# Gated linear attention on one core: inverse norms of q spread over the partitions by DMA instead of TensorE transposes

## The reference

```python
q = l2norm((x @ Wq).reshape(B, T, 8, 128))      # u / max(sqrt(sum(u*u)), 1e-12), per head and position
k = l2norm((x @ Wk).reshape(B, T, 8, 128))
v = (x @ Wv).reshape(B, T, 8, 128)
alpha = sigmoid(x @ Wg).reshape(B, T, 8, 128)
# for each t:  S = alpha_t * S + k_t v_t^T ;  o_t = S^T q_t
x = layernorm(x + o @ Wo)
x = layernorm(x + ffn(x))
```

## Time and profile before

| what | value |
|---|---|
| median of 3 runs | 1853.79 us (1848.47 to 1857.78) |
| the profiled execution | 1857.98 us |
| its span, first to last instruction | 1856.2 us |
| PE busy | 1725.2 us, 93% of the span |
| DVE busy | 1462.5 us, 79% |
| ACT busy | 1077.9 us, 58% |
| POOL busy | 600.1 us, 32% |
| chain of work that ended last | PE 77%, DVE 11%, issue 6%, ACT 4%, DMA 0% |
| mean granted PE clock | 0.987 of full |
| SP's DMAs in the attention | 16 loads of x_nat, 256 KB each, median 3.5 us to landing |

### The profile page before, as it was taken

How to read it: one execution, slowest core, us unless ns; L and a number is a source line. 1 busy time by engine, 2 the same in 40 slices (tenths; PEclk the granted TensorE clock), 3 DMA queues, 4 the chain that set the end, 5 groups by cost and what they waited for, 6 DMA issues and landing times.

```text
span 1856.2 us, 81900 instructions
## 1 busy us (share of the span) xinstructions
PE 1725.2 (93%) x35719; PEld 1425.5 (77%) x35719; DVE 1462.5 (79%) x3391; ACT 1077.9 (58%) x2355; POOL 600.1 (32%) x474
## 2 busy tenths in 40 slices
PE   6999999999999999999999999999789999999996
PEld 5788887878878788887878888878667777777775
DVE  4878887888888778787887888788768787878786
ACT  5665555656656655665566566555455656565553
POOL 2322222232223223222322322232234444444444
PEclk9999999999999999999999999999989999999999
DMA  7000000000000000000000000000000000000000
GB/s 211 4 10 9 4 9 4 10 4 9 10 4 9 4 9 4 9 9 4 9 4 9 4 10 9 4 9 3 3 12 13 22 20 16 24 12 24 13 17 12
DMA packets 28657, 26.99 MB, mean 15 GB/s; under 512 B 1928, under 2 KB 23696, under 8 KB 28304
## 3 DMA queue, kind: packets, MB, share of 16 engines
q1 hardware_dynamic: 28304, 21.77, 3.9%
HBM read 13.38 MB, written 4.19 MB: 9 GB/s over the span
## 4 chain that ended last, share of the span: by engine, by line
PE 77%; DVE 11%; issue 6%; ACT 4%; DMA 0%; POOL 0%; DVEq 0%; SPq 0%; POOLq 0%; ACTq 0%
PE bank L527 11%; PE bank L529 10%; PE bank L528 10%; PE bank L660 8%; PE bank L615 7%; PE bank L670 5%; PE bank L646 5%; PE bank L618 5%; PE bank L567 5%; PE bank L577 4%; PE bank L634 3%; PE bank L603 3%; ACT v_sb L979 2%; DVE v_sb L1531 2%; DVE s_sb L1528 1%
## 5 line engine op out<-in xcount | busy, mean ns | idle before, releaser
L458 POOL TENSOR_TENSOR rn_sb<-ss_sb,expo 128x8 f32<-128x8 f32 x128 | 213.4, 1668 | 783.2 <-DVE ss_sb L1287 783.2
L1242 DVE TENSOR_TENSOR qq_sb<-qq_sb,tot_sb 128x512 f32<-128x512 f32 (+1 forms) x384 | 264.2, 688 | 189.5 <-PE bank L615 150.1
L1242 DVE TENSOR_TENSOR k_sb<-k_sb,tot_sb 128x512 f32<-128x512 f32 (+1 forms) x384 | 322.8, 841 | 4.7 <-PE bank L618 4.5
L1004 ACT ACTIVATE at_sb<-diag_sb 32x256 f32<-32x256 f32 x256 | 106.0, 414 | 171.6 <-DVE diag_sb L1254 166.9
L979 ACT ACTIVATE v_sb<-bank,rn_sb 128x128 f32<-128x128 f32 x512 | 139.1, 382 | 82.0 <-PE bank L529 78.5
L615 PEld LDWEIGHTS bank<-qq_sb,k_sb 128*32 128x32 f32 x12288 | 128.6, 110 | 59.6 <-issue 44.9
L615 PE MATMUL bank<-qq_sb,k_sb 128*32 128x16 f32 x12288 | 149.7, 185 | 23.2 <-issue 21.6
L968 ACT ACTIVATE a_sb<-bank 128x512 f32<-128x512 f32 x128 | 76.3, 597 | 154.1 <-PE bank L529 145.7
L660 PE MATMUL bank<-v_sb,at_sb 128*128 128x128 f32 x1024 | 151.6, 291 | 4.4 <-DVE res L1294 2.5
L495 POOL TENSOR_TENSOR wq_lo<-v_sb,wq_hi 128x512 fp32r<-128x512 f32 x80 | 104.7, 1308 | 138.0 <-ACT wq_hi L1127 138.0
L1120 ACT ACTIVATE sq_sb<-bank 128x512 f32<-128x512 f32 x160 | 95.4, 597 | 86.2 <-PE bank L529 85.7
(11 more groups left out here) (203 smaller groups left out, 4366.2 us busy)
## 6 DMA issues: line engine op xcount, KB each, us to landing
x_nat<-in_L_attn_x_dram SPq DMA_DIRECT2D x16, 256.0 KB, 3.5
x_nat<-x_all SPq DMA_DIRECT2D x16, 256.0 KB, 2.4
out_dram<-k_sb SPq DMA_DIRECT2D x16, 256.0 KB, 2.3
ew_raw<-in_L_ffn_exp_w_dram SPq DMA_DIRECT2D x3, 512.0 KB, 5.0
qq_sb<-in_L_attn_Wq_dram SPq DMA_DIRECT2D x1, 512.0 KB, 4.1
qq_sb<-in_L_attn_Wk_dram SPq DMA_DIRECT2D x1, 512.0 KB, 6.4
k_sb<-in_L_attn_Wg_dram SPq DMA_DIRECT2D x1, 512.0 KB, 7.2
k_sb<-in_L_attn_Wv_dram SPq DMA_DIRECT2D x1, 512.0 KB
```

The source lines that it names most:

```text
L458: nc.gpsimd.tensor_tensor(rn_sb[par][:, i, :, :].rearrange("p h c -> p (h c)"), ss_sb[:, i * G:(i + 1) * G], expo[:, 0:G], ALU.pow).then_i ...
L1242: return nc.vector.tensor_tensor(view, view, by, ALU.mult)
```

## The change

The eight transposes of a slot become one: PE transposes the 128 x 8 tile `rn_sb` as it is into 8 rows of 128 (`turn_norms`), ACT copies these 8 x 128 numbers into `nr_sb` (`take_norms`), SP stores them as 4 KB in memory (`nr_dram`), waits for that, and loads the 4 KB back into each of the 128 partitions of `nb_sb` (512 KB written). DVE then multiplies all of q by `nb_sb` in one instruction of 128 x 1024, now placed behind the growth for j = 6. The load of x for later batches is issued from the same SP loop, no longer from a loop of its own.

```diff
+        nr_sb = sb("nr_sb", [G, C])
+        nb_sb = sb("nb_sb", [128, W])
+        nr_dram = nc.dram_tensor("nr_dram", (2, G, C), fp32, kind="Internal").ap()
...
-            with sp.Fori(1, B) as b:
-                next_x(b)
+            def spread_norms(P):
+
+                rows = nr_dram[P % 2]
+                sp.wait_ge(rr_evac, P + 1)
+                sp.dma_start(rows, nr_sb[:, :]).then_inc(nr_out, 16)
+                sp.wait_ge(nr_out, (P + 1) * 16)
+                await_count(sp, qn_done, P)
+                sp.dma_start(nb_sb[:, :], bass.AP(rows.tensor, rows.offset, [[0, 128], [1, W]])).then_inc(nr_in, 16)
+
+            for P in range(B * NP):
+                spread_norms(P)
+                if P == 0:
+                    next_x(1)
+                if P % NP == NP - 1 and P // NP + 2 < B:
+                    next_x(P // NP + 2)
...
-            def spread_norms(par, P):
+            def turn_norms(par, P):
 
                 pe.wait_ge(rn_done, P * 2 + 1)
-                await_count(pe, s_done, (P - 1) * HP * (NC - 1))
-                for h, bank in enumerate((nb_ps, kt_ps)):
-                    for c in range(NC):
-                        mm = nc.tensor.transpose(bank[:, c * C:(c + 1) * C],
-                                                 rn_sb[par][:, 0, h, c:c + 1].to_broadcast([128, 128]), ident[:, :])
-                    mm.then_inc(rb_full, 1)
+                nc.tensor.transpose(nb_ps[0:G, C:2 * C], rn_sb[par][:, 0, :, :].rearrange("p h c -> p (h c)"), ident[:, :]).then_inc(rr_full, 1)
...
                     scores(par, P, 5)
+                    if has_next:
+                        turn_norms(1 - par, P + 1)
                     if has_prev:
                         outputs_of_state(prev_p, P - 1, 0)
                     if has_next:
                         sums_of_squares(P + 1, 1, n_x)
-                        spread_norms(1 - par, P + 1)
                     scores(par, P, 6)
...
+            def take_norms(P):
+
+                act.wait_ge(rr_full, P + 1)
+                await_count(act, nr_out, P * 16)
+                nc.scalar.activation(nr_sb[:, :], nb_ps[0:G, C:2 * C], ACT.Copy).then_inc(rr_evac, 1)
...
                         take_gate(1 - par, P + 1)
+                        take_norms(P + 1)
                     spread_diagonal(par, P)
...
-            def normalise_q(par, P, h):
-                dve.wait_ge(rb_full, P * HP + h + 1)
-                seg = q_sb[par][:, h * T:(h + 1) * T]
-                nc.vector.tensor_tensor(seg, seg, (nb_ps, kt_ps)[h][:, :], ALU.mult).then_inc(qn_done, 1)
+            def normalise_q(par, P):
+                dve.wait_ge(nr_in, (P + 1) * 16)
+                nc.vector.tensor_tensor(q_sb[par][:, :], q_sb[par][:, :], nb_sb[:, :], ALU.mult).then_inc(qn_done, 1)
...
-                        if j == 6 and has_next:
-                            for h in range(HP):
-                                normalise_q(1 - par, P + 1, h)
-
...
                     if has_next:
+                        normalise_q(1 - par, P + 1)
                         own_products(1 - par, P + 1)
```

More of the change, by code:

```diff
@@ L226, in gated_linear_attention_and_moe_block @@
         rn_done = sem("rn_done")
-        rb_full = sem("rb_full")
+        rr_full = sem("rr_full")
+        rr_evac = sem("rr_evac")
+        nr_out = sem("nr_out")
+        nr_in = sem("nr_in")
         qn_done = sem("qn_done")
@@ L369, in next_x @@
                 sp.wait_ge(xt_full, b)
-                sp.dma_start(x_nat[:, :, :], x[bass.ds(b, 1)].rearrange("a (c t) d -> t (a c) d", t=C)).then_inc(xn_in, 16)
-            with sp.Fori(1, B) as b:
-                next_x(b)
+                sp.dma_start(x_nat[:, :, :], x[b].rearrange("(c t) d -> t c d", t=C)).then_inc(xn_in, 16)
+            def spread_norms(P):
[11 more added lines that the diff above has]
+                    next_x(P // NP + 2)
             def ffn_io(b, first=False, last=False):
@@ L514, in transposes_of_x @@
                 pe.wait_ge(xn_in, (n + 1) * 16)
-                await_count(pe, qn_done, n * NP * HP - 1)
+                await_count(pe, rr_evac, n * NP)
                 for c in range(NC):
@@ L557, in sums_of_squares @@
                     pe.wait_ge(x_lo, n_x)
-                    await_count(pe, qn_done, P * HP)
+                    await_count(pe, rr_evac, P)
                 else:
@@ L626, in transposes_of_k @@
                     pe.wait_ge(k_up, (P + 1) * 6)
-                    if not last:
-                        pe.wait_ge(qn_done, (P + 2) * HP)
+                    await_count(pe, s_done, P * HP * (NC - 1))
                 else:
@@ L723, in _ @@
             sums_of_squares(0, 1, 1)
-            spread_norms(0, 0)
+            turn_norms(0, 0)
             for n in range(2):
@@ L1041, in _ @@
             take_gate(0, 0)
+            take_norms(0)
             for n in range(2):
@@ L1210, in own_products @@
             def own_products(par, P):
-                dve.wait_ge(qn_done, (P + 1) * HP)
+                dve.wait_ge(qn_done, P + 1)
                 await_count(dve, qk_full, (P - 1) * STEPS + 1)
@@ L1358, in _ @@
             dve.wait_ge(const_dve, 5)
-            for h in range(HP):
-                normalise_q(0, 0, h)
+            normalise_q(0, 0)
             own_products(0, 0)
```

## The result

| | before | after |
|---|---|---|
| median | 1854.66 us (4 runs) | 1917.89 us (4 runs, 1911.08 to 1923.22) |
| profiled span | 1856.2 us | 1914.0 us |
| mean granted PE clock | 0.987 | 0.975 |

The ratio is 1.0343, 95% interval [1.0299, 1.0387]: slower by 63 us, where +48 was forecast; the time lies inside the range.

What follows compares the result with a forecast made beforehand. PE was taken to bound the kernel. Slots +29, work queued behind DVE's wait +7 and the start +12 summed to +48 us: 1906 us profiled, 1902 us against the median, range 1855 to 1985.

Steps and rivals of the forecast that it cites:

- allowance: Time in a slot between PE's turning of the norms and `scores(1)` of the next slot: mean 9.27 us.
- The new chain: From the turn through store, load and DVE to `scores(1)`: 9.73 us, 0.46 us longer than the allowance.
- 29 + 7: Costs given to slots: 29 us for the longer chain, 7 us for work queued behind DVE's wait.
- PE's own work: Seven of eight transposes go, 0.89 us a slot, leaving PE's path from turn to `scores(1)` at 8.38 us.
- The trip hides: Rival: store and load together cost 3.5 us instead of 5.0, PE stays the bound, 1814 us; chance 0.07.
- W + R: W, the store without its bytes, 1.56 us, plus R, the load into 128 partitions, 3.44 us.
- Its neighbour: Rival: W + R between 4.1 and 4.5 us, time about 1858 us or just below; chance 0.07.
- The one-row read is slow: Rival: loading the same 4 KB into all 128 partitions takes 5.1 us, total 2007 us; chance 0.13.
- DVE and POOL get in each other's way: Rival: the new multiplication loses 0.42 us beside a POOL product, +26 us, 1928 us; chance 0.05.
- The place on DVE: DVE's growths of j = 6 are no part of the chain, ending near 619 us, norms arriving near 620.1.
- Queued behind DVE's wait: DVE instructions behind the normalisation delay a new batch's first projection by 0.5 us in 15 slots, +7 us.
- The start: The first store of norms stands behind all the starting loads on SP: first `scores(1)` at 45.5 us, +12 us.

Runs made afterwards that it cites:

- e7: The changed kernel, its load bringing only the first head's norms (256 KB), which scale both heads: 1900.93 us, ratio 1.0208.
- e2: The changed kernel without the store of the norms and its wait; the load reads 4 KB of Wq instead: 1857.31 us, ratio 1.0030.
- e10: e9 with seven transposes a slot put back on PE, whose result nobody reads: 1876.29 us, ratio 1.0080.
- e6: The changed kernel, its load taking 128 different rows of Wq instead of one row for all partitions: 1921.35 us, ratio 1.0329.
- e3: The changed kernel with the turning transpose moved ahead of the second half of the gates' projection: 1863.08 us, ratio 1.0080.
- e9: The changed kernel with the edits of e1 and e3 together: 1870.89 us, ratio 1.0048.
- e8: The changed kernel with the normalisation back ahead of the growths of j = 6: 2011.06 us, ratio 1.0826.
- e4: The kernel before, with only its normalisation moved behind the growths of j = 6: 1849.93 us, ratio 1.0004.
- e1: The changed kernel, with the norms of slot 0 alone spread by the eight transposes of before: 1903.13 us, ratio 1.0286.
- e12: The kernel before, with sums of squares over 128 positions at once instead of four times 32: 1933.77 us, ratio 1.0408.
- e11: e9 with sums of squares over 128 positions at once instead of four times 32: 1910.40 us, ratio 1.0288.
- e5: The changed kernel with the store of the norms issued twice in series, each awaited: 2030.52 us, ratio 1.0931.

## Why the prediction was right, and where it was off

**What bounds the kernel.** Right. The kernel was bound by PE with a short DVE tail behind the norms, and the trip through memory became the chain that sets `scores(1)`. The allowance of 9.27 us from four slots is 9.22 over all 62.

**The new chain.** Means over 62 slots, the forecast by the prediction's own terms:

| step, us | forecast | measured |
|---|---|---|
| turn to the store's issue | 0.27 + 0.28 + 0.17 | 0.60 |
| store to the load's issue | 1.56 + 0.17 | 1.51 |
| load to the normalisation | 3.44 + 0.05 | 3.72 |
| normalisation to `scores(1)` | 1.20 + 2.49 + 0.10 | 4.07 |
| sum | 9.73 | 9.90 |

Each step is within 0.3 us. The store had the right sum by luck: 1.24 with its hop in 46 of 64 slots, 2.3 on average in the other 18. The load's 3.44 was near (3.6), but its parts weren't: e7 shows 0.4 for 256 KB, not 0.74, so more of it is fixed. DVE's part was 0.3 short; `scores(1)` came 3.91 after the normalisation in the median slot, not 3.79, and later where POOL's product was met. The forecast was +0.46 a slot; the slot grew by 0.63, 39 us against the 29 + 7 I gave to slots. That these two sums are so near is in part luck: of the 7 only 3 came, and the 6 that the part up to the outputs grew by were not in the sum.

**PE's own work.** This is the step that failed, though it left the sum alone, since DVE ends last. I priced eight transposes at 0.89 us a slot, called PE's gain certain, and let `scores(6)` come 0.89 earlier. From the first outputs to `scores(6)` the mean went from 2.91 to 2.35 us only, the median from 2.53 to 2.31. Before, `scores(6)` started 0.46 us (median) after DVE's growth of k for j = 5 had ended; the least that any kernel shows is 0.10. So there was 0.36 us of slack behind that growth, and PE now waits out the rest in 39 of 60 slots; the whole 0.89 counts only where a gap behind an instruction packet had made PE late, which is why the mean fell by more than the median. The growth takes 1.53 us beside POOL's first product of the gates in both kernels. Where the trip hides (e2), a third of a microsecond is lost again behind `scores(6)` (6.64 us to `scores(1)`, 6.31 before), where the normalisation now meets POOL, and the slots gain 0.22. Putting the work back (e10) costs 0.1 a slot by the medians, 0.19 in the profile. I also wrote that the wait at the edge would hide PE's "issue" gaps; those behind instruction packets went only from 41.9 to 37.0 us. And since PE loses part of its gain before the edge, it waits there 0.9 us a slot (55 us in 60), not the 1.3 I named as a sign.

**The rivals.** "The trip hides" needed W + R under 4.2. It was 1.34 + 3.6 = 4.9, and even at 3.7 (e2) the time is 1857 and not 1814, because PE waits for DVE ahead of `scores(6)` and of `scores(1)` instead. Its neighbour, W + R from 4.1 to 4.5, was put at 1858 or just below; at 4.5 my own terms give -0.04 x 63 + 19 = +16, 1870. "The one-row read is slow" falls by e6. "DVE and POOL get in each other's way" happens in 18 of 63 slots of the change, at 0.38 us each, 7 us in all and not 26: in the others POOL's product has ended before the norms arrive, as I said, or ends within 0.2 us of it. In e2, e3 and e9 it is nearly every slot. The rule of a fixed 2.0 us and bytes / 436e3 would have 2.01 for the store and 3.20 for the load, estimates from the Trainium skill, "DMA: Bandwidth & Descriptors", section "Anatomy of one DMA — SWDGE (gpsimd) path". That section is on DMAs issued by GpSimd, which I didn't say, and these are issued by SP. Here the store's issue to the load's is 1.24, and the load is 3.6. For 256 KB the rule says 0.6, e7 0.4.

**The place on DVE.** That the growths of j = 6 are no part of the chain is right: with them in it (e8) the time is 90 us more, and the move by itself costs nothing (e4).

**Queued behind DVE's wait.** The first projection of a new batch starts 1.65 us after `scores(1)`, 1.44 before (15 slots each): +0.21, 3 us in all where I said 7. What covers the rest of the four DVE instructions I did not resolve. The delayed masks cost nothing that shows: the part of the slot up to the outputs grew by 0.10, as much as the turn now ahead of them takes (0.11 from 647.01 to the outputs).

**The start.** Forecast 45.5 and +12 (9 to 14), measured 45.12 and +13.4; e1 takes it away. The store did wait for the loads ahead of it.

**What was not in the sum.** The second half, "untouched", took 5.2 us longer: the same code at a granted clock of 0.97, 0.98 before. 13.4 + 39.2 + 5.2 = 57.8 us is the whole difference of the spans. The medians are 63 apart; the rest is from run to run.

## What to carry to other kernels

A spread over partitions by a store of 4 KB and a load of 512 KB costs 5 us from the first issue to landing, so it must start that long before its use, or not at all on an edge where the slack is 1 us. Before work is taken off a busy engine, look at what the next instruction behind it waits for: 0.89 us taken off ahead of an instruction with 0.36 us of slack brings no more than the slack, unless something else had delayed the engine. A wait marked "issue" is one without a name, not one for instructions; compare where it ends with the ends of the other engines' work. Idle work put back tells quickly how much of a saving is real, and the place of the gap that it fills tells where the rest went. And put independent work into the wait, not behind it: the same two instructions were worth 90 us with the trip and nothing without.

## What the runs showed of the hardware

**PE waits behind instruction packets.** The DMA engines also carry PE's instructions. The pages list 284 instruction packets of 16 KB in queue q8 before, 280 after and 236 in e12, where PE has 35719, 35271 and 29575 matmuls: one packet for 250 to 252 matmuls and weight loads in each (as many loads as matmuls). Before, 73 of PE's 91 gaps marked "issue" in 50 to 1310 us end 1.1 to 1.7 us after such a packet has ended, 41.9 of 46.3 us; only 12% of all moments lie so. In the slot above, the packet ends at 647.51 and the gap in the sums of squares at 648.95. Most stand in or ahead of rows of short matmuls, and with 96 of these fewer a slot (e11, e12) none is left. That PE runs out of instructions there fits both; no run delays a packet to show it alone.

**Instruction packets and small stores.** Behind the start, the slowest store took 3.10 us to the load's issue. SP's timeline and the DMA queues (packets, MB, share of 16 engines) from 142 to 146 us, after:

```profile
142.54 0.28 SPq L382 DMA_DIRECT2D nr_dram<-nr_sb  x1
145.64 0.32 SPq L385 DMA_DIRECT2D nb_sb<-nr_dram  x1
```

```profile
q8 instruction: 1, 0.02, 1.8%
q1 hardware_dynamic: 16, 0.00, 0.6%
```

The one instruction packet took 1.8% of 16 engines in 4 us, 1.15 us. In 16 of the 18 slow slots an instruction packet (of q8, or of the smaller q14) was in flight between 0.90 and 1.25 us after the issue, while an undisturbed store ends, but also in 22 of the 46 others. That it delays the store where both fall on one engine would fit; no run tests it.

**Clock and waits go together.** The granted clock of these traces is either full (2.4 GHz) or half (1.2 GHz), and what is given here is the mean of a stretch. Over all executions, the median of the whole kernel is 0.988 to 0.989 before and 0.977 after; it is 0.982 in e9, 0.988 in e10 with the idle transposes, 0.958 in e8 and 0.953 in e5, where PE waits longest. In the 120 us behind the first slots it was 0.99 before (66 to 186 us) and 0.96 after (80 to 200). The second half is the same code everywhere: it took 536.7 to 538.5 us at 0.98 before and in e4 and e10, and 541.0 to 542.7 at 0.97 after and in e1, e2, e5, e7 and e9. e3, e8, e11 and e12 lie between (539.4 to 540.1), and e6 is an exception with 538.6 at 0.97. These are single executions, so that waits of PE in the first half cost microseconds in the second is likely, not shown.

**One moving column.** 16 matmuls of 128 x 128 for the sums took 1.84 us in e12; the 64 of 128 x 32 that do the same take 0.71 before. I had expected 0.3 to 0.4 us more for such a group and it took 1.1, so it cost both kernels more than the gaps it closed.
